# Cross-attention and mixture-of-experts layers on one core: the key stacks put behind the first gather, the context load among the expert pairs, the first maxima two steps later

## The reference, cut to what matters

```
x = x + L0_xattn(layernorm(x), ctx, itok)      # 16 heads, keys limited to a window of 9
x = x + L0_ffn(layernorm(x))                   # shared expert + top 2 of 8 experts
x = x + L1_xattn(layernorm(x), ctx)            # 16 heads of 16, all 1601 keys, int8 fake-quant
x = x + L1_ffn(layernorm(x))

# L1_xattn
q = _qdq(x) @ _qdq(wq).T + bq
kv = cond @ wkv.T + bkv
attn = softmax(einsum('bnhd,bmhd->bhnm', q, k) * scale)
out = _qdq(einsum('bhnm,bmhd->bnhd', attn, v)) @ _qdq(wp).T + bp
```

## Time and profile before

| | us |
|---|---|
| median of 3 runs | 808.86 |
| lowest and highest | 806.12, 809.22 |
| profiled execution, its own time | 805.29 |
| its span | 803.2 |
| TensorE busy | 725.5 (90%) |
| VectorE busy | 555.4 (69%) |
| ScalarE busy | 380.6 (47%) |
| GpSimd busy | 208.5 (26%) |
| mean granted TensorE clock | 0.963 |

### The profile page before, as it was taken

One profiled execution on the slowest core, in us unless ns is written; L12 is line 12 of the kernel. 1 busy time (PEld: TensorE's weight loads), 2 busy tenths in 40 slices (PEclk: granted clock), 3 DMA queues, 4 the chain that ended last, 5 costly groups with the idle time before them and its releaser, 6 DMA issues.

```text
span 803.2 us, 13098 instructions
## 1 busy us (share of the span) xinstructions
PE 725.5 (90%) x4986; PEld 423.1 (53%) x4987; DVE 555.4 (69%) x1209; ACT 380.6 (47%) x521; POOL 208.5 (26%) x206
## 2 busy tenths in 40 slices
PE   8999899979897787878979999989999999899996
PEld 4446676846686564334434455544455554445434
DVE  4887987625372435777878787777787777887814
ACT  2102334346432230345756665556665566664670
POOL 2497232312651211123400505001505002300000
PEclk9999999999899796789999999999999999999999
DMA  9900001004589435922764491814491810560000
GB/s 293 341 0 1 1 1 48 35 1 180 166 251 234 123 75 100 141 72 40 128 78 69 151 108 62 119 20 60 161 108 54 122 23 2 114 72 15 1 1 14
DMA packets 42185, 71.96 MB, mean 90 GB/s; under 512 B 6309, under 2 KB 29989, under 8 KB 41222
## 3 DMA queue, kind: packets, MB, share of 16 engines
q1 hardware_dynamic: 39384, 60.34, 35.3%
q0 software_dynamic: 2592, 9.12, 4.5%
q10 hardware_dynamic: 144, 1.64, 0.6%
HBM read 48.66 MB, written 22.42 MB: 88 GB/s over the span
## 4 chain that ended last, share of the span: by engine, by line
PE 58%; DVE 16%; issue 13%; DMA 7%; ACT 3%; POOL 2%; SPq 1%; POOLq 0%; DVEq 0%
PE ps L1278 10%; PE ps L1362 9%; PE ps L1342 7%; PE ps L1082 5%; PE ps L1092 4%; DVE small L2061 4%; PE ps L961 3%; DMA y<-yscr,pos 3%; DMA yscr<-r 2%; PE ps L1008 2%; PE ps L1193 2%; PE ps L1051 2%; PE ps L968 2%; PE ps L1039 2%; DVE small L1875 1%
## 5 line engine op out<-in xcount | busy, mean ns | idle before, releaser
L2061 DVE TENSOR_REDUCE small<-ps 128x1 f32<-128x400 f32 (+1 forms) x512 | 284.6, 572 | 92.2 <-PE ps L1278 86.1
L1736 ACT ACTIVATE r<-ps 128x1024 f32<-128x1024 f32 (+1 forms) x208 | 212.5, 1023 | 103.6 <-PE ps L1342 100.7
L1278 PE MATMUL ps<-r 96*128 96x400 bf16 (+1 forms) x512 | 173.8, 347 | 26.7 <-DVE small L2061 16.7
L1362 PE MATMUL ps<-r 128*17 128x256 f32 (+1 forms) x1664 | 132.4, 391 | 1.6 <-ACT r L1736 1.3
L1342 PE MATMUL ps<-r 99*128 99x256 bf16 (+1 forms) x832 | 128.8, 278 | 0.7 <-ACT r L1714 0.7
L1278 PEld LDWEIGHTS ps<-r 96*128 96x128 bf16 x512 | 50.3, 98 | 142.0 <-DVE small L2061 99.9
L1342 PEld LDWEIGHTS ps<-r 99*128 99x128 bf16 (+1 forms) x832 | 82.5, 101 | 33.3 <-issue 10.2
L849 POOL TENSOR_TENSOR r<-r 128x401 bf16<-128x401 f32 (+3 forms) x72 | 66.0, 950 | 105.1 <-ACT r L1586 104.1
L1092 PE MATMUL ps<-wkvT,r 128*128 128x256 f32 (+1 forms) x208 | 59.6, 403 | 2.6 <-ACT r L1597 2.2
L1362 PEld LDWEIGHTS ps<-r 128*17 128x17 f32 (+1 forms) x1664 | 27.8, 96 | 52.2 <-issue 42.4
L1082 PE MATMUL ps<-r,wkvT 128*128 128x400 f32 (+1 forms) x128 | 52.5, 506 | 2.4 <-issue 2.0
(11 more groups left out here) (247 smaller groups left out, 954.1 us busy)
## 6 DMA issues: line engine op xcount, KB each, us to landing
r<-kscr SPq DMA_DIRECT2D x84, 200.1 KB, 8.7
kscr<-r SPq DMA_DIRECT2D x18, 400.2 KB, 3.6
r<-in_ctx_dram SPq DMA_DIRECT2D x3, 1601.0 KB
r<-xscr SPq DMA_DIRECT2D x14, 256.0 KB, 3.8
yscr<-r SPq DMA_DIRECT2D x14, 256.0 KB, 5.0
r<-qscr SPq DMA_DIRECT2D x24, 128.0 KB, 5.2
xscr<-hT SPq DMA_DIRECT2D x1, 2432.0 KB, 21.7
kscr<-r POOLq DMA_DIRECT2D x6, 400.2 KB, 8.7
```

The costliest lines, as they stand in the source:

```text
L1278: mm(bank(ca % 2)[:, 0:m], qst[0:SROWS, h, q0:q0 + P], kst[0:SROWS, s % 2, h % HALF, a:a + m], start=True, stop=True).then_inc(mx_mm, 1)
L1362: last = mm(bank(6)[32 * k:32 * k + VW, 0:LQ], vx[0:n, b % 2, kt, h, :], pr[i % 3][0:n, k * LQ:(k + 1) * LQ], start=kt == 0, stop=kt == KT ...
L1736: fn(pr[i % 3][0:n, :], bank(2 + 2 * (i % 2), 2)[0:n, :], ACT.Exp, scale=SCALE1)\
L2061: v.tensor_reduce(mxc[quad % 2][:, n:n + 1], bank(ca % 2)[:, 0:m], AX_X, ALU.max).then_inc(mx_rdy, 1)
```

## The change

Four things are moved. On POOL, both stages' keys are written first (`write_keys(0)`, `write_keys(1)`), then comes `fetch(0)`, then the stack of quad 0; the stack of quad 1 comes behind `split_queries(0)`. A stack of quad 0 or 1 now waits for 96 on the write semaphore, both stages, where it waited for 48. On ACT, the load of batch 1's context (1.6 MB) is issued ahead of step 13 of the pairs, where it stood ahead of step 0. The 32 maxima of quad 0 stand in steps 21 to 27 of the pairs, seven steps, where they stood in 19 to 24, six. The join of batch 1 stands in step 26 of the pairs where it stood in step 0 of the scores, that of batch 2 at step 0 where it stood at 4, that of batch 3 at step 4 where it stood at 9. Line numbers of the changed kernel are 3 higher from here on.

```
-JOINS = (None, 0, 4, 9)
+JOINS = (None, None, 0, 4)
...
-FSTEPS = FIRST_V + (KT + 1) // 2
-FIRST_MAX = NI
+FIRST_MAX = NI + 2
+FSTEPS = FIRST_MAX + 7
+FIRST_JOIN = FIRST_MAX + 5
+CONTEXT = NI - 6
...
-    for b in range(1, B):
+    for b in range(2, B):
         put(JOINS[b], "query", b, "join")
...
+    beside.setdefault(FIRST_JOIN, []).append(("query", 1, "join"))
...
-            eng.wait_ge(*key_parts_out(s))
+            eng.wait_ge(*key_parts_out(max(s, 1)))
...
             write_keys(pool, 0)
+            write_keys(pool, 1)
+            fetch(0)
             stack_quad(pool, 0)
-            write_keys(pool, 1)
-            stack_quad(pool, 1)
-            fetch(0)
             rsqrt_query(0)
             split_queries(0)
+            stack_quad(pool, 1)
             fetch(1)
             fetch(2)
             rsqrt_query(1)
...
-            act.dma_start(ctxT, ctx_in[1]).then_inc(ld_ctx, 16)
-
...
             for n in range(FSTEPS):
+                if n == CONTEXT:
+                    act.dma_start(ctxT, ctx_in[1]).then_inc(ld_ctx, 16)
```

## The result

| | us |
|---|---|
| before, median of 20 runs | 808.16 |
| changed, median of 20 runs | 814.67 (809.20 to 821.78) |
| ratio | 1.0086, 95% interval 1.0061 to 1.0112 |

The change makes the kernel slower by 6.5 us; 815 was forecast.

The account below looks back on a forecast made before the run. PE, 90% busy, was taken as the bound, its waits mattering. Batch 0's 10.3 us gain shrinks to +0.1 at nst; +3.4, +4.4 and -1.4 at the later joins make +6.4 us: 815 us, range 804 to 823.

Parts of the forecast that it names:

- The join of batch 0: In the pairs: with writes and fetch ahead of the stacks, this join ends at 260.3 us, 10.3 us earlier.
- From the join to the split queries: After batch 0's join: the 22.4 us to the split stay as they were, queries split at 282.8 us.
- rival B: Pairs, steps 15 and 16: stack of quad 0 and context load delay rows, everything behind 5 us later, 820 us; chance 0.15.
- The stack ahead of the queries: Quad 1's stack beside SP's query write: split to landed queries grows from 12.1 to 21.6 us, a stack costing 9.5.
- Rival A: POOL's stack does not hold up SP's queue; queries land at 294.9 us, total 803 us; chance 0.15.
- C: Rival: the stack holds the queries up by half, 4.7 us; total 810 to 811 us; chance 0.20.
- The join of batch 1: Late in the pairs: gathers from 307.2 to 325.9 us, join ends at 327.3, nst at 329.7, before 329.6.
- The joins of batches 2 and 3: Scores, steps 0 and 4: DVE waits 3.4 and 7.6 us for gathers; joins end at 339.5 and 356.2 us.
- The sum: Whole kernel: all terms net to +6.4 us, giving 811.7 on the profiled execution and 815 as median.
- Nothing later takes it back: After the score joins: the delay stays to the end, since PE is then the engine that is always busy.

Follow-up runs that it names:

- e5_fetch3: Changed kernel with the gathers of batch 3 issued ahead of the power of batch 1 in POOL's queue; ratio to the kernel before 1.0004.
- e6_joins_ctx: Changed kernel with the context load back at step 0 of the pairs and the joins of batches 2 and 3 back at steps 4 and 9; ratio 0.9927.
- e8_stack1_sp: Changed kernel with the context load early, joins of batches 2 and 3 at steps 4 and 9, stack of quad 1 in SP's queue; 796.63 us, ratio 0.9859.
- b2_pool: Kernel before with only POOL's order taken from the changed kernel; joins, first maxima and context load as before; ratio 0.9940.
- e1_joins: Changed kernel with the joins of batches 2 and 3 back at steps 4 and 9 of the scores; 807.39 us, ratio 0.9972.
- e9_sp_only: Changed kernel with one edit, the stack of quad 1 in SP's queue behind the last stores; ratio to the kernel before 1.0107.
- e4_ctx: Changed kernel with the load of batch 1's context back ahead of step 0 of the pairs; ratio to the kernel before 1.0097.
- a2_again: Changed kernel run again unedited, giving its second profiled execution; ratio to the kernel before 1.0124.

## Why the prediction was right, point by point

**The join of batch 0** was put at 260.3 us and ends at 260.5. Right in size and cause: the first gather starts 12.7 us earlier, and PE's 5.1 us go, but for 1.2. The size is that of an execution without the stall at 219 to 232 us: the four traces that have POOL's new order and no stall end this join at 259.5 to 261.9 us, the eight with it at 263.9 to 268.7, the changed kernel's first execution at 266.1.

**From the join to the split queries** I kept 22.4 us. This term is mis-sized. In four traces with POOL's new order and a single stack there (`e5_fetch3`, `e6_joins_ctx`, `e8_stack1_sp`, `b2_pool`) it takes 19.7 to 19.8 us, with no wait for rows and a mean clock of 1.00. The changed kernel takes 23.9 us in the second execution and 21.4 in the first. Two things go with the longer times. One is a pair's rows: one load of them takes 14.27 us, beside the stack and the context load, which I had costed at nothing; PE waits 1.2 us for it, and the clock over the step is 0.86. Such a wait is in three of the five traces with the late load and a single stack (0.2 and 0.3 us in `e1_joins` and `e9_sp_only`) and in none of the four with the early one. The other is a clock of 0.92 without any wait for rows, at 21.4 us: this is in the changed kernel's first execution, but also in `e4_ctx`, where the load is early, so it isn't the load's, and its cause is open. The errors lie on opposite sides, and the forecast 282.8 stands beside 284.4, by luck. So rival B was there, at 1.2 us instead of 5; at 13 us once a second stack is added.

**The stack ahead of the queries** was to make 12.1 into 21.6 us. Seven traces with a stack there have 18.2 to 20.5 us, seven without 11.0 to 12.3: the means are 19.7 and 11.9. The delay is 7.8 us. SP's reads of the queries are issued 9.1 to 11.0 us after the writes in the seven with the stack and 2.9 us after in the seven without, so it is the writes that are held up. The mechanism is shown, the term of 9.5 us 1.7 us too large. Rival A (none) is out, C (4.7) too small. The Trainium skill's page "DMA: Bandwidth & Descriptors", by whose "Anatomy of one DMA — SWDGE (gpsimd) path" I had estimated 4.8 us for a stack, is further from the measurement than the 9.5 us of the earlier trace rows; my estimate counted the six transfers of a stack as one.

**The join of batch 1**: gathers from 306.5 to 324.3 us, forecast 307.2 to 325.9. `nst` at 327.95, forecast 329.7. The low clock that I had taken over from the earlier trace rows has moved: at 305 to 314 us it is 0.93 in place of 0.50, but from 320 to 340 us it is 0.50, where the kernel before has 0.78. The sum has no term for this second dip. `e1_joins` has 0.50 there too with a block of 34 us, so the dip alone doesn't make the block long.

**The joins of batches 2 and 3**: DVE was to wait 3.4 and 7.6 us and waits 3.47 and 6.67; the joins were to end at 339.5 and 356.2 and end at 338.1 and 354.4. From `nst` of quad 0 to that of quad 1 the forecast is 6.3 us more than before (3.4 + 4.4 - 1.4, less the 0.1); measured are 6.9 in the second execution and 8.1 in the first. `e5_fetch3` shows by taking it away that the second wait is POOL's order, and `e1_joins` that without the two placings the block is not only back at 37 but at 34 us, since the join of batch 1 is no longer in it. I had not said this: there were 3 us to win there.

**The sum.** At `nst` of quad 1 the changed kernel's second execution is 5.2 us behind before (372.69 and 367.48), forecast 6.4, and the medians are 6.5 apart. The first execution is 10.8 us behind there; the 5.6 us between the two executions are already there at the end of batch 0's join. The second profiled execution ends 10.4 us behind, as it loses another 1.3 to 1.6 us three times, each where the granted clock falls for some microseconds:

```profile
450.00:460.00 10.00, 8.37 (x73) 3.73 (x66) 7.58 (x14) 5.76 (x6) 7.85 (x9) 0.83 0.23 93
690.00:700.00 10.00, 8.39 (x68) 3.64 (x67) 7.71 (x15) 5.11 (x7) 6.26 (x7) 0.83 0.29 112
745.00:755.00 10.00, 8.39 (x62) 3.96 (x60) 6.68 (x17) 4.36 (x5) 0.00 (x0) 0.83 0.09 29
```

"Nothing later takes it back" was right, but later stretches are not neutral: `b2_pool`, too, has 7.1 us of gain up to 686 us and 3.0 after, with a clock of 0.59 from 680 to 692 us. Why these dips fall where they do was not tried. That the total agrees within a microsecond is therefore partly luck; what held are the mechanisms and the size of the two waits.

By parts, against the kernel before: POOL's order alone -0.6%; the joins of batches 2 and 3 at their early steps +1.1 to +1.7 (from `e1_joins` and the changed kernel, and from `e4_ctx` and `e6_joins_ctx`); the first maxima and the join of batch 1 in the pairs near nothing (`b2_pool` and `e6_joins_ctx`, of different sets). The late context load is +0.7% in the kernel before, where it meets the gathers of batch 0; in the changed kernel the comparisons give between nothing (`e4_ctx`) and 0.5 (`e1_joins` and `e6_joins_ctx`), none of it clear of the intervals.

## What to carry to other kernels

A consumer in an in-order queue can be put no earlier than its data: before a join is moved up, add up what its gathers wait for, including what merely stands ahead of them in the issuing queue (here a power that wanted a later step), and remember that everything behind the join waits with it. A bulk transfer is moved to where nothing urgent follows, and queue order alone does not protect the urgent one: 1.2 MB on one queue held up small transfers on another by 8 us, and beside the pairs' rows two of them made one pair 9 to 13 us late. The bytes in flight count (without the 1.6 MB of context the wait is 4.4 us shorter); whether the issuing queue counts as well was not tried, as no run puts a stack at the same moment into another queue. When two such faults lie one behind the other, mending the first shows little until the second is mended: from the first write of the queries to `nst` of quad 1, moving stack 1 into SP's queue gives 2.4 us with the joins early (88.3 us in `a2_again`, 85.9 in `e9_sp_only`) and 8.2 us with them late (79.7 in `e6_joins_ctx`, 71.5 in `e8_stack1_sp`). The ratios point the same way, 0.2 and 0.7 points, but their intervals overlap.

## What the runs showed of the hardware that I had not expected

In some executions PE and ACT stand still together for 2 to 6 us in one piece between 219 and 232 us, in most of them with `remote` as ACT's releaser, which is another core or a queue that the profile doesn't know; ACT in the first execution of the changed kernel:

```profile
226.16 0.60 ACT L1643 ACTIVATE r<-ps 128x512 f32<-128x512 f32 x1 [2.74 <-remote]
227.59 0.39 ACT L1649 ACTIVATE r<-ps 128x256 f32<-128x256 f32 x1 [0.84 <-remote]
```

What ACT waits for in the first row, PE had finished 2.7 us earlier (its transposes end at 223.4 us). SP's next transfer is issued at 226.15 us, together with ACT's row. The stall was in the first execution of the changed kernel and in all eight traces of the first two sets, and in none of the four of the last; its cause is open.

Indirect gathers of 128 rows took POOL 1.25 us each to issue, and four of them took 7.5 to 8.0 us from ready to landed in light traffic, 10.2 to 10.8 us among a few stacks and up to 18.7 us among many (the earlier trace rows and above).
